# Four graph layers on one Trainium2 core: the turned attention weights of odd tiles are copied out of PSUM by VectorE instead of ScalarE

## The chip, the cores and the metric

The kernel runs on one NeuronCore of a Trainium2 chip. The metric is the device time of one execution in microseconds (us). Five engines work beside each other, each through its own instruction queue in order: TensorE (PE in the profile), VectorE (DVE), ScalarE (ACT), GpSimd (POOL) and SyncE (SP, which issues DMAs here). They wait for each other through semaphores.

## The reference

For each of 8 graphs of 1024 nodes with 128 features, four layers follow each other. Each adds its output to its input and normalizes the rows (layer norm).

```python
x = _layernorm(x + _L0_gnn_ref(adj, x, ...))   # max over the first 25 neighbours, then a linear layer
x = _layernorm(x + _L1_gnn_ref(x, adj, ...))   # graph attention
x = _layernorm(x + _L2_gnn_ref(x, adj, ...))   # graph attention
x = _layernorm(x + _L3_gnn_ref(x, adj, ...))   # attention with logits q x^T, two steps
```

The last layer is the one that the change touches:

```python
mask = jnp.where(dep_adjs == 1, 0.0, NEG)
q = jnp.einsum('bnh,hk->bnk', inputs, att_W)
score = jnp.einsum('bnk,bmk->bnm', q, inputs) / jnp.sqrt(H)
att_adjs = jax.nn.softmax(score + mask, axis=-1)
for W, b in ((W0, b0), (W1, b1)):
    xw = jnp.einsum('bnh,hk->bnk', x, W) + b
    x = jnp.tanh(jnp.einsum('bnm,bmk->bnk', att_adjs, xw))
```

## The kernel before

The 8 graphs are numbered 0 to 7 here. A graph's 1024 nodes are 8 tiles of 128 rows. While graph b goes through its four layers, the neighbour search of graph b+1 (layer 0's maximum) is done in the gaps, by a fixed order written out by hand in each engine's queue. It has two ways for each tile. Some neighbours are gathered from memory: `gather` on POOL issues one indirect DMA a slot (L565), each followed by a small memset as a pause (L570), 18 slots in tiles 0 to 3 and 17 in tiles 4 to 7. They land in a ring of three tile buffers, so a tile's gather waits until the tile three before it has been reduced on DVE (`pool_tile`, L1331 and L1332, `rows_pooled`), and it needs row indices that DVE computes (`find_keys`, `find_members`, `rows_ready`). The other neighbours are "picked" on PE: `pick(b + 1, q)` for q = 0 to 14 is 16 matmuls (L905) with a one-hot matrix that DVE (`make_hot`, L1379) or ACT (`make_hot`, L634 and L637) builds; DVE then takes the maximum (`max_pick`, L1391), which frees the PSUM bank for the next pick. `side_work` runs DVE's share of the search at named places, among them "tile 1" to "tile 5" inside the attention loop, and "steps", "last step", "half" and "end" behind it. In "steps" stand `pool_tile` of tile 4, and `find_keys` and `find_members` of graph b+2. "last step" is `pool_tile` of tile 5, "half" that of tile 6, "end" that of tile 7.

The last layer turns the attention weights tile by tile. For tile t:

- PE multiplies queries by keys into `low` or `high` by turns (L1111) and adds the mask (L1115), and raises `logits_psum`.
- DVE takes the row maximum (L1535), and raises `row_max`.
- ACT takes the exponential with the row sum into `work` (L747, `att_exp`), prepares the mask of tile t+2 (`narrow`, L597), and copies the turned tile t-2 from PSUM (`side_t`) into `probs_t` (L754, `att_t_ready`).
- PE turns tile t-2 with 8 transposes (L1129, `att_turned`) into `side_t`. There is one `side_t`: it must have been copied before the next tile is turned.

PE's order in its loop of 10 steps is: at t = 2 pick 9 and at t = 6 pick 10, the logits of t, then (t = 8, 9) `attend` for two tiles, then the turn of tile t-2. `attend(t)` (L1089) is 8 matmuls that multiply the turned weights with the values. Behind the loop come `attend(4)` to `attend(7)`. Then the first step's result goes through tanh on ACT (L761; it needs `recip`, the reciprocals of the row sums, L1545 on DVE), is turned by `turn_first(0)` and `turn_first(1)` (L1097) with pick 11 around them, is projected (L937), pick 12 follows, and then the second step (L1154) with pick 13 inside, and tanh on ACT (L776). ACT's order behind its loop is: one-hot of pick 11 (L634 and L637, twice), wait for `recip_ready`, tanh. DVE's order behind its loop is: `recip`, "steps", `max_pick` 11, one-hot of pick 12, "last step", `max_pick` 12, and then the residual and statistics of the second step.

Of the kernel before, what the change touches and what calls it, by code (L numbers as in the profile page):

```python
# [19 lines left out]
P = 128  # L20
# [146 lines left out]
def build_graph_layers(nc, x, adj, w0, b0, w1, b1, a1, w2, a2, watt, w3a, b3a, w3b, b3b, out):  # L167
# [13 lines left out]
    with ExitStack() as ctx:  # L181
# [6 lines left out]
        def signal(name, per, unit=1, ahead=0, first=None):  # L188
            return Signal(ctx, nc, name, per, unit, ahead, first)
# [204 lines left out]
        row_max = signal("row_max", T)  # L394
        att_exp = signal("att_exp", T)
        att_turned = signal("att_turned", T)
        att_t_ready = signal("att_t_ready", T)
        recip_ready = signal("recip_ready", 1)
        att_heads = signal("att_heads", 4)
        first_turned = signal("first_turned", 2)  # L400
# [179 lines left out]
        def _(act):  # L580
# [142 lines left out]
            def graph(b, slot, in_loop):  # L723
# [18 lines left out]
                for t in range(T + 2):  # L742
                    if t < T:
                        act.wait_ge(row_max.sem, row_max.at(b, t + 1))
                        if t >= 3:
                            act.wait_ge(att_turned.sem, att_turned.at(b, t - 2))
                        att_exp.raised_by(nc.scalar.activation(work[:, t % 3, :], (low, high)[t % 2], ACT.Exp,  # L747
                                                               bias=neg_max[:, t:t + 1],
                                                               accum_out=row_sum[:, t:t + 1]))
                        if t + 2 < T:  # L750
                            narrow(b, t + 2, place)
                    if t >= 2:
                        act.wait_ge(att_turned.sem, att_turned.at(b, t - 1))
                        att_t_ready.raised_by(nc.scalar.copy(probs_t[:, :, (t - 2) * P:(t - 1) * P], side_t))  # L754
                if exists(b, 1, B, in_loop):
                    make_hot(b + 1, 11)
                act.wait_ge(recip_ready.sem, recip_ready.at(b, 1))
# [71 lines left out]
        def _(pe):  # L829
# [208 lines left out]
            def graph(b, slot, in_loop):  # L1038
# [61 lines left out]
                for t in range(T + 2):  # L1100
                    if t == 2 and exists(b, 1, B, in_loop):
                        spare_maxed(b + 1, 8)
                        pick(b + 1, 9)
                    if t == 6 and exists(b, 1, B, in_loop):
                        spare_maxed(b + 1, 9)
                        pick(b + 1, 10)
                    if t < T:
                        if t >= 2:
                            pe.wait_ge(att_exp.sem, att_exp.at(b, t - 1))
                        for half in halves:  # L1110
                            nc.tensor.matmul((low, high)[t % 2][:, half], queries[:, t * P:(t + 1) * P],  # L1111
                                             xt[:, half], start=True, stop=False, skip_group_check=True)
                        pe.wait_ge(adj_narrowed.sem, adj_narrowed.at(b, t + 1))
                        for half in halves:
                            last = nc.tensor.matmul((low, high)[t % 2][:, half], ident_masked[:, :],  # L1115
                                                    adj_less_1[:, t % 2, half], start=False, stop=True,
                                                    skip_group_check=True)
                        logits_psum.raised_by(last)
                    if t == T:
                        pe.wait_ge(att_exp.sem, att_exp.at(b, T - 1))  # L1120
                    if t >= T:
                        for i in range(2 * (t - T), 2 * (t - T) + 2):
                            attend(i)
                    if t >= 2:
                        pe.wait_ge(att_exp.sem, att_exp.at(b, t - 1))
                        if t >= 3:
                            pe.wait_ge(att_t_ready.sem, att_t_ready.at(b, t - 2))
                        for m in range(T):
                            last = nc.tensor.transpose(side_t[:, m, :], work[:, (t - 2) % 3, m * P:(m + 1) * P],  # L1129
                                                       ident[:, :])  # L1130
                        att_turned.raised_by(last)
                for t in range(4, T):
                    if t == T - 1:
                        pe.wait_ge(att_t_ready.sem, att_t_ready.at(b, T))
                    attend(t)
                turn_first(0)
                if exists(b, 1, B, in_loop):
# [78 lines left out]
        def _(dve):  # L1216
# [290 lines left out]
            def graph(b, slot, in_loop):  # L1507
# [21 lines left out]
                    max_pick(b + 1, 8)  # L1529
                    make_hot(b + 1, 9)  # L1530
                side_work(b, slot, "attention", in_loop)
                for t in range(T + 1):
                    if t < T:
                        dve.wait_ge(logits_psum.sem, logits_psum.at(b, t + 1))
                        row_max.raised_by(nc.vector.tensor_reduce(neg_max[:, t:t + 1], (low, high)[t % 2], AX.X,  # L1535
                                                                  ALU.max, negate=True))
                    if f"tile {t}" in SIDE:
                        side_work(b, slot, f"tile {t}", in_loop)
                    if t == 4 and picks:
                        max_pick(b + 1, 9)  # L1540
                        make_hot(b + 1, 10)
                    if t == T and picks:
                        max_pick(b + 1, 10)
# [106 lines left out]
```

## Time and profile before

| what | value |
| --- | --- |
| median of 3 runs | 1954.62 us (1948.86 to 1959.94) |
| profiled execution | 1953.58 us |
| its span, first to last instruction | 1951.8 us |
| mean granted TensorE clock | 0.94 of full |
| busy share PE, DVE, ACT, POOL | 85%, 72%, 58%, 75% |

The span is what the trace covers; the profiled execution's time is 1.8 us more. A graph takes 225 us in the steady part. Times in rows are counted from the start of the span. The attention loops of graphs 0 to 7 begin near 320, 548, 772, 999, 1223, 1448, 1677 and 1879 us. POOL gathers for graph 7 until 1761 us, and has nothing to do in graph 7 itself.

### The profile page before, as it was taken

The page shows a single profiled execution, that of the slowest core. Times are in us where ns is not written, and L with a number is a line of the kernel's source. Part 1 is how long each engine was busy: PE and PEld are TensorE (multiplying, and loading weights), DVE is VectorE, ACT ScalarE, POOL GpSimd, SP SyncE. Part 2 cuts the span into 40 slices and gives each one's busy share as a digit, 9 for nine tenths or more (in the row PEclk, how much of TensorE's full clock was granted, in tenths as well). Part 3 has the DMA queues.
Part 4 walks back from the last instruction along what each step waited for, and adds up shares of the span by engine and source line. Part 5 has one row for each costly group of instructions (what it writes and reads, how often), then busy time and mean ns, then how long its engine had stood idle before and what let it go on. Part 6 is the DMA issues. An engine that isn't in the chain of part 4 may idle for free.

```text
span 1951.8 us, 29181 instructions
## 1 busy us (share of the span) xinstructions
PE 1666.7 (85%) x9655; PEld 1308.6 (67%) x9700; DVE 1413.3 (72%) x3406; ACT 1126.7 (58%) x1517; POOL 1471.4 (75%) x2191
## 2 busy tenths in 40 slices
PE   4777898979889899899989899997988899896877
PEld 2655675757758577677748677675767687584746
DVE  5874888668876788668885788758886688745631
ACT  5665756646665765657566565558556565652252
POOL 6888888888888887888788887888888887880000
PEclk9989899989999899998999899998999899997889
DMA  7231433343342333334233432434333422311020
GB/s 194 71 83 45 106 75 110 87 107 76 77 131 75 101 78 94 109 91 118 76 115 75 113 78 75 126 77 112 83 101 86 131 55 64 107 43 38 1 65 11
DMA packets 154177, 168.88 MB, mean 87 GB/s; under 512 B 103133, under 2 KB 120426, under 8 KB 154026
## 3 DMA queue, kind: packets, MB, share of 16 engines
q1 hardware_dynamic: 119594, 96.43, 18.2%
q0 software_dynamic: 34432, 70.59, 14.1%
q8 instruction: 76, 1.25, 0.3%
q14 instruction: 75, 0.61, 0.1%
HBM read 142.29 MB, written 4.19 MB: 75 GB/s over the span
## 4 chain that ended last, share of the span: by engine, by line
POOL 32%; PE 31%; DVE 17%; issue 9%; ACT 5%; DVEq 4%; DMA 2%; POOLq 0%; ACTq 0%; SPq 0%
POOL gathered L565 24%; POOL pause L570 8%; PE big L1013 7%; PE spare L905 6%; PE big L937 4%; DVE pooled L1331 3%; DVEq L73 2%; DVE probs_t L1458 2%; PE big L1004 2%; PE big L1154 1%; PE big L1089 1%; DVE keys L1228 1%; ACT hot L634 1%; PE big L1111 1%; PE big L995 1%
## 5 line engine op out<-in xcount | busy, mean ns | idle before, releaser
L565 POOL DMA_INDIRECT gathered<-in_x_dram,rows x1076 | 1107.1, 1029 | 246.9 <-issue 163.3
L905 PE MATMUL spare<-hot,x_part 128*128 128x512 f32 x1440 | 366.7, 407 | 28.5 <-DVE hot L1379 18.9
L570 POOL MEMSET pause<- 32x256 bf16 x1076 | 357.6, 332 | 42.0
L905 PEld LDWEIGHTS spare<-hot,x_part 128*128 128x128 f32 x1440 | 271.3, 194 | 94.7 <-issue 19.4
L634 ACT ACTIVATE hot<-running,minus_count 128x2048 fp32r<-128x2048 bf16 (+1 forms) x131 | 250.8, 1914 | 85.1 <-PE spare L905 65.0
L637 ACT ACTIVATE hot<-hot,plus_one 128x2048 fp32r<-128x2048 f32 (+1 forms) x131 | 251.4, 1919 | 4.3
L1331 DVE TENSOR_REDUCE pooled<-gathered 128x128 f32<-128x2176 f32 (+2 forms) x56 | 218.2, 3897 | 32.0 <-DMA gathered<-in_x_dram,rows 30.5
L1013 PEld LDWEIGHTS big<-values,probs_t 128*128 128x128 f32 x1792 | 224.7, 203 | 8.5
L1013 PE MATMUL big<-values,probs_t 128*128 128x129 f32 x1792 | 227.7, 288 | 0.4
L1379 DVE TENSOR_SCALAR hot<-running 128x2048 fp32r<-128x2048 bf16 (+1 forms) x131 | 167.6, 1302 | 26.5 <-PE big L905 11.7
L1458 DVE SCALAR_TENSOR_TENSOR probs_t<-side,col_gain,adj_t 128x1024 f32<-128x1024 f32 x128 | 154.6, 1276 | 27.2 <-ACT side L693 27.2
L1535 DVE TENSOR_REDUCE neg_max<-big 128x1 f32<-128x1024 f32 x64 | 78.2, 1222 | 99.5 <-PE big L1115 99.5
L615 ACT CAST running<-spare 128x512 bf16<-128x512 f32 x92 | 53.8, 585 | 150.3 <-remote 84.2
L905 PE MATMUL side<-hot,x_part 128*128 128x512 f32 x448 | 115.6, 403 | 26.9 <-DVE hot L1379 16.9
L1111 PE MATMUL big<-xt,queries 128*128 128x512 f32 x256 | 121.1, 595 | 6.5 <-ACT values L679 6.1
L747 ACT ACTIVATE work<-big,neg_max 128x1024 f32<-128x1024 f32 x64 | 71.3, 1114 | 95.1 <-DVE neg_max L1535 95.1
L1089 PE MATMUL big<-values,probs_t 128*128 128x128 f32 x1024 | 118.3, 275 | 0.0
L1154 PEld LDWEIGHTS big<-values,probs_t 128*128 128x128 f32 x1024 | 116.6, 192 | 2.0 <-ACT values L679 0.9
L905 PEld LDWEIGHTS side<-hot,x_part 128*128 128x128 f32 x448 | 80.4, 188 | 55.8 <-issue 16.6
L1154 PE MATMUL big<-values,probs_t 128*128 128x128 f32 x1024 | 116.8, 275 | 0.7 <-ACT values L679 0.7
L1089 PEld LDWEIGHTS big<-values,probs_t 128*128 128x128 f32 x1024 | 116.2, 192 | 0.0
L1391 DVE TENSOR_TENSOR best_t<-best_t,spare 128x512 f32<-128x512 f32 x75 | 51.6, 688 | 77.4 <-PE spare L905 71.2
(203 smaller groups left out, 2613.8 us busy)
## 6 DMA issues: line engine op xcount, KB each, us to landing
adj_in<-in_adj_dram SPq DMA_DIRECT2D x128, 512.0 KB
gathered<-in_x_dram,rows POOLq DMA_INDIRECT x1076, 2.5
xs<-in_x_dram SPq DMA_DIRECT2D x8, 512.0 KB, 4.7
out_dram<-xs SPq DMA_DIRECT2D x8, 512.0 KB, 3.2
adj_t<-adj_bf SPq DMA_TRANSPOSE x64
packed_t<-group_bits SPq DMA_TRANSPOSE x28, 2.7
w_sb<-in_L_gnn_W_dram SPq DMA_DIRECT2D x1, 128.0 KB
w_sb<-in_L_gnn_W_dram SPq DMA_DIRECT2D x2, 64.0 KB
```

Of the source, the lines that this page charges most:

```text
L565: (late_gathered if late else rows_gathered[t % RING]).raised_by(pool.indirect_dma_start(out=gathered[:, t % RING, k * C:(k + 1) * C], out ...
L570: last = nc.gpsimd.memset(pause[quarter:quarter + 32, k // (4 * PAUSED), :], 0.0)
L634: hot_apart.raised_by(nc.scalar.activation(chunk, running[:, tiles[0]:tiles[-1] + 1, :], ACT.Abs, bias=minus_count[:, s:s + 1]))
L637: hot_made.raised_by(nc.scalar.activation(chunk, chunk.bitcast(F32), ACT.Relu, scale=-1.0, bias=plus_one[:, 0:1]))
L905: last = nc.tensor.matmul(pick_bank(b, q), x_parts[part][:, m, :], hot[:, place_of(b, q, m), :], start=(m == 0 and part == 0), stop=(m == ...
L1013: last = nc.tensor.matmul(heads[:, t, 0:C + 1], probs_t[:, j, t * P:(t + 1) * P], values[:, j, :], start=False, stop=(j == T - 1), skip_gr ...
L1089: last = nc.tensor.matmul(low_t[:, t, :], probs_t[:, m, t * P:(t + 1) * P], values[:, m, 0:C], start=(m == 0), stop=(m == T - 1))
L1111: nc.tensor.matmul((low, high)[t % 2][:, half], queries[:, t * P:(t + 1) * P], xt[:, half], start=True, stop=False, skip_group_check=True)
L1154: last = nc.tensor.matmul(low_t[:, t, :], probs_t[:, m, t * P:(t + 1) * P], values[:, m, 0:C], start=(m == 0), stop=(m == T - 1))
L1331: link(nc.vector.tensor_reduce(pooled[:, t, :], rows_of[:, :, 0:n], AX.X, ALU.max))
L1379: hot_ready.raised_by(nc.vector.tensor_scalar(hot_chunk(b, q, c), running[:, tiles[0]:tiles[-1] + 1, :], float(wanted(b, q)), None, ALU.is ...
L1458: gat_probs.raised_by(nc.vector.scalar_tensor_tensor(out=probs_t[:, j, :], in0=gains, scalar=col_gain[:, j:j + 1], in1=adj_t[slot][:, j, : ...
```

## The change

At each odd step t >= 3 of the loop, the copy of tile t-2 is taken from ACT's queue and put into DVE's queue, behind the row maximum of t and ahead of DVE's side work at that step. The semaphore `att_t_ready` becomes two, one for even tiles (raised by ACT) and one for odd tiles (raised by DVE). DVE's loop becomes one step longer: at t = 9 it waits for the turn of tile 7 and copies it, ahead of `recip`.

```diff
-        att_t_ready = signal("att_t_ready", T)
+        att_t_ready = [signal(f"att_t_ready{i}", T // 2) for i in range(2)]
...
-                    if t >= 2:
+                    if t >= 2 and t % 2 == 0:
                         act.wait_ge(att_turned.sem, att_turned.at(b, t - 1))
-                        att_t_ready.raised_by(nc.scalar.copy(probs_t[:, :, (t - 2) * P:(t - 1) * P], side_t))
+                        att_t_ready[0].raised_by(nc.scalar.copy(probs_t[:, :, (t - 2) * P:(t - 1) * P], side_t))
...
                         if t >= 3:
-                            pe.wait_ge(att_t_ready.sem, att_t_ready.at(b, t - 2))
+                            copied = att_t_ready[(t - 3) % 2]
+                            pe.wait_ge(copied.sem, copied.at(b, (t - 3) // 2 + 1))
...
                     if t == T - 1:
-                        pe.wait_ge(att_t_ready.sem, att_t_ready.at(b, T))
+                        pe.wait_ge(att_t_ready[1].sem, att_t_ready[1].at(b, T // 2))
...
-                for t in range(T + 1):
+                for t in range(T + 2):
                     if t < T:
                         dve.wait_ge(logits_psum.sem, logits_psum.at(b, t + 1))
                         row_max.raised_by(nc.vector.tensor_reduce(neg_max[:, t:t + 1], (low, high)[t % 2], AX.X,
                                                                   ALU.max, negate=True))
+                    if t >= 3 and t % 2 == 1:
+                        dve.wait_ge(att_turned.sem, att_turned.at(b, t - 1))
+                        att_t_ready[1].raised_by(nc.vector.tensor_copy(probs_t[:, :, (t - 2) * P:(t - 1) * P], side_t))
                     if f"tile {t}" in SIDE:
                         side_work(b, slot, f"tile {t}", in_loop)
```

## Rows read from the trace of the kernel before

**Rows 1.** Page, the chain of work that ended last, by engine.

```profile
POOL 32%; PE 31%; DVE 17%; issue 9%; ACT 5%; DVEq 4%; DMA 2%; POOLq 0%; ACTq 0%; SPq 0%
```

**Rows 2.** Timeline, POOL: start us, us, instruction, [idle before <- releaser]; tile 4 for graph 4.

```profile
978.51 1.06 POOL L565 DMA_INDIRECT gathered<-in_x_dram,rows  x1 [6.21 <-DVE pooled L1332]
```

**Rows 3.** Timeline, DVE: reduction of tile 7 in graphs 0, 3, 4, 5.

```profile
414.17 3.79 DVE L1331 TENSOR_REDUCE pooled<-gathered 128x128 f32<-128x2176 f32 x1 [8.87 <-DMA gathered<-in_x_dram,rows]
...
1087.95 3.90 DVE L1331 TENSOR_REDUCE pooled<-gathered 128x128 f32<-128x2176 f32 x1 [0.92 <-DMA gathered<-in_x_dram,rows]
...
1315.68 3.90 DVE L1331 TENSOR_REDUCE pooled<-gathered 128x128 f32<-128x2176 f32 x1 [3.78 <-DMA gathered<-in_x_dram,rows]
...
1538.21 3.90 DVE L1331 TENSOR_REDUCE pooled<-gathered 128x128 f32<-128x2176 f32 x1 [3.67 <-DMA gathered<-in_x_dram,rows]
```

**Rows 4.** Timeline, DVE, graph 3: row maxima of tiles 3, 4; last index rows; reciprocals.

```profile
1014.10 1.22 DVE L1535 TENSOR_REDUCE neg_max<-big 128x1 f32<-128x1024 f32 x1
...
1018.29 1.22 DVE L1535 TENSOR_REDUCE neg_max<-big 128x1 f32<-128x1024 f32 x1 [1.34 <-PE big L1115]
...
1027.19 0.26 DVE L1298 TENSOR_SCALAR rows<-row_f,row_base 128x34 uint32<-128x34 f32 x1
...
1035.78 0.20 DVE L1545 RECIPROCAL recip<-row_sum 128x8 f32<-128x8 f32 x1 [0.49 <-ACT work L747]
```

**Rows 5.** Timeline, PE: graph 3's turns of tiles 1, 7, turn_first(0), pick 12; graph 5's turn_first(0).

```profile
1015.04 1.07 PE L1129 MATMUL side<-ident,work 128*128 128x128 f32 x8 [1.56 <-ACT probs_t L754]
...
1042.69 1.04 PE L1129 MATMUL side<-ident,work 128*128 128x128 f32 x8
...
1053.72 0.66 PE L1097 MATMUL side<-ident,work 128*128 128x128 f32 x4 [2.85 <-ACT work L761]
...
1062.35 3.90 PE L905 MATMUL spare<-hot,x_part 128*128 128x512 f32 x16
...
1502.79 0.66 PE L1097 MATMUL side<-ident,work 128*128 128x128 f32 x4 [2.85 <-ACT work L761]
```

**Rows 6.** Lines by form: one-hot on DVE; copies from PSUM on ACT and DVE.

```profile
L1379 DVE TENSOR_SCALAR hot<-running 128x2048 fp32r<-128x2048 bf16 x105 | 127.8, 1245 | 0.3
...
L754 ACT COPY probs_t<-side 128x1024 f32<-128x1024 f32 x64 | 64.2, 1003 | 48.8 <-PE side L1129 48.8
...
L1389 DVE COPY best_t<-spare 128x512 f32<-128x512 f32 x15 | 10.4, 691 | 2.7 <-issue 0.9 <-PE spare L905 0.7
```

**Rows 7.** Timeline, DVE: max_pick 11 in graphs 1, 3, 5.

```profile
609.42 0.69 DVE L1391 TENSOR_TENSOR best_t<-best_t,spare 128x512 f32<-128x512 f32 x1 [8.25 <-PE spare L905]
...
1060.12 0.69 DVE L1391 TENSOR_TENSOR best_t<-best_t,spare 128x512 f32<-128x512 f32 x1 [7.60 <-PE spare L905]
...
1507.61 0.69 DVE L1391 TENSOR_TENSOR best_t<-best_t,spare 128x512 f32<-128x512 f32 x1 [6.67 <-PE spare L905]
```

**Rows 8.** Timeline, ACT, graph 3: the one-hot of pick 11 starts.

```profile
1044.67 2.01 ACT L634 ACTIVATE hot<-running,minus_count 128x2048 fp32r<-128x2048 bf16 x1
```

**Rows 9.** Windows: pick 11 of graphs 3 and 5; the third figure from the end is PEclk.

```profile
1054.00:1060.00 6.00, 6.00 (x24) 4.57 (x22) 0.00 (x0) 1.76 (x5) 4.64 (x7) 0.72 0.17 44
1503.00:1508.00 5.00, 5.00 (x26) 3.61 (x24) 0.39 (x1) 1.83 (x5) 4.26 (x7) 1.00 0.21 52
```

**Rows 10.** Graph 6: last late reduction on DVE; last gather on POOL; median landing.

```profile
1765.32 1.45 DVE L1324 TENSOR_REDUCE pooled<-gathered 128x128 f32<-128x768 f32 x1
...
1760.52 0.95 POOL L565 DMA_INDIRECT gathered<-in_x_dram,rows  x1 [0.16 <-issue]
...
gathered<-in_x_dram,rows POOLq DMA_INDIRECT x1076, 2.5
```

**Rows 11.** Timeline, PE, graph 7: turns of tiles 2 and 3.

```profile
1892.28 1.06 PE L1129 MATMUL side<-ident,work 128*128 128x128 f32 x8
...
1897.02 1.06 PE L1129 MATMUL side<-ident,work 128*128 128x128 f32 x8 [1.53 <-ACT probs_t L754]
```

**Rows 12.** Timeline, POOL, graph 3: a gather during DVE's one-hot of pick 10.

```profile
1022.99 2.29 POOL L565 DMA_INDIRECT gathered<-in_x_dram,rows  x1 [0.16 <-issue]
```

## The prediction, made before the changed kernel was built or run

> **What bounds the kernel now.** I read the page's chain first, then the chain in order of time, then the timelines of PE, DVE, ACT and POOL through the attention of graphs 0, 3, 6 and 7, and last the idle times that stand at the same two places in every graph. The chain gives POOL 32% and ACT only 5% [rows 1]. In order of time it splits each steady graph in two. From the moment DVE reduces tile 1 of the next graph (behind layer 2), POOL gathers tiles 4 to 7 without a gap, for about 107 to 110 us. POOL has waited for that reduction, 6.21 us in this row [rows 2], and it waits at that place in each of the graphs 1 to 6. The whole attention layer lies beside that stretch. It ends when the last rows of tile 7 land and DVE, which is already there, reduces them [rows 3]. From there to the next release of POOL the path is DVE and PE.
>
> So in graphs 0 to 5 the attention costs nothing as long as DVE arrives at tile 7 before its data. The reader should see in [rows 3] how much is left: 8.87 us in graph 0, but only 0.92 us in graph 3 (graphs 1 and 2 are within 0.1 of it), and 3.78 and 3.67 in graphs 4 and 5. A gain in the attention of graphs 0 to 5 is worth nothing, a delay above these margins is paid in full, and it is not given back, since POOL then waits for DVE. In graph 6 the path runs through PE and ACT up to tile 7. Graph 7 has no gathers, and its attention is on the path as a whole.
>
> **What is moved, and its price.** 32 copies leave ACT, 4 a graph, at 1.00 us each [rows 6]. DVE has no copy of this size. Its copy of 512 elements from PSUM takes 0.69, so the bound above is 1.38. Its maximum over 1024 elements from PSUM takes 1.22 [rows 4], which is the nearest row in size and I take it. The bound below is the ACT copy's 1.00.
>
> **Inside the loop.** In graph 3 DVE ends the row maximum of tile 3 at 1015.32 and would go on with side work, but the turn of tile 1 ends at 1016.11 [rows 4, 5]. Wait and copy take it to 1017.33, 2.0 us later. 1.34 us of this was idle before the maximum of tile 4 [rows 4], so 0.7 is left (0.45 to 0.7 over the graphs; I take 0.6). It moves logits, pick 10 and all that follows in the loop. Tiles 3 and 5 have been turned, or nearly, when DVE comes to them; their copies fit into its idle time. DVE's last index rows of the next graph move from 1027.45 to about 1029.4, and POOL asks for them only near 1033 (its tile 6), so that is hidden.
>
> What ACT gives up in the loop is no gain. The chain goes through the copies of tiles 0, 2 and 4, which stay on ACT. Graph 7, where nothing is done beside the loop, shows it: the turn of tile 2 starts without waiting for the copy of odd tile 1, the turn of tile 3 waits 1.53 us for the copy of even tile 2 [rows 11]. With a copy of 1.22 on DVE I walk through the loop of graph 7 and find every later turn where it was. Graph 7: 0.
>
> **Behind the loop: the wait that counts.** DVE reached `recip` at 1035.78. Now it must first wait for the turn of tile 7, which ends at 1043.73 [rows 4, 5], plus 0.6 from above, plus the copy of 1.22: `recip` comes near 1045.6, 9.8 us later. The turn is late since PE does `attend(0)` to `attend(3)` around it. Queued behind it on DVE are `recip`, "steps" (reduction, keys and members), `max_pick` 11, and the one-hot of pick 12. Before, DVE idled 8.25, 7.60 and 6.67 us ahead of `max_pick` 11 in graphs 1, 3 and 5 [rows 7]; graph 2 is like 1, graph 4 like 3. So `max_pick` 11 is late by 1.5, 1.5, 2.2, 2.1 and 3.1 us in graphs 1 to 5. Maximum and first half of the one-hot took 0.69 and 1.25 [rows 6, 7], so that half was ready near 1062.0, and PE started pick 12 at 1062.35 [rows 5]: 0.4 of the delay is absorbed: pick 12 is late by 1.1, 1.1, 1.8, 1.7 and 2.7.
>
> ACT wins on the other side. Without the copy of tile 7 it starts the one-hot of pick 11 near 1040.9 in place of 1044.67 [rows 8], and tanh behind it as much earlier. `recip` at 1045.6 is then not what it waits for. PE's wait of 2.85 us ahead of `turn_first(0)` [rows 5] goes, and PE is through with pick 11 and the projection about 4 us early. It then stands before pick 12 for some 5 us, until DVE has the one-hot. The early ACT is worth nothing here: the stall has moved from 1051 to 1059 and grown.
>
> **The clock.** The wait of 2.85 us before pick 11 was followed by a mean granted clock of 0.72 in graph 3, a part of the stretch at 1.2 GHz and the rest at 2.4, and of 1.00 in graph 5, all at 2.4 [rows 9]. From `turn_first(0)` to `max_pick` 11 it was 6.40 us in graph 3 and 4.82 in graph 5 [rows 5, 7]: 1.6 us is the price of the lower clock. Graphs 1 to 4 and 6 paid it, 0 and 5 did not. The new idle time of 5 us is longer, so I expect the 1.2 GHz behind it in all graphs, now in pick 12, where nothing absorbs it. With 1.6 more the second step is late by 2.7, 2.7, 3.4, 3.3 and 4.3. Less the margins of [rows 3] the tile 7 reduction is late by 1.8, 1.8, 2.5, 0 and 0.6 us in graphs 1 to 5. Graph 0 has 8.87 and nothing is left of its 5: 0. Sum: +6.7.
>
> **Graph 6.** There is no graph 8, so "steps" is only the reduction, and DVE has far more idle time than it loses. PE keeps what ACT gave it: 2.85 - 0.6, and 1.3 since the lower clock goes, 3.6 in all. At its end the last six rows of tile 7 stand in the way: issued at 1760.52 and 2.5 later landed, so near 1763.2, where DVE reduced them at 1765.32 [rows 10]. Gain 2.1 of the 3.6.
>
> Total: +6.7 - 2.1 = +4.6 on the profiled execution's 1953.58 (span 1951.8 and 1.8 around it), 1958.2. The median of the runs is 1.0 above that execution, so the changed kernel's median would be up to 1959.2; I put 1958.5.
>
> **A rule against the change.** A gather of POOL takes 0.95 us, and 2.29 when DVE's one-hot (bf16 in SBUF to SBUF) runs beside it [rows 12]. The rows around DVE's copies and maxima from PSUM show 0.95. If the new copy held POOL like the one-hot, each would cost up to 1.3 us of a POOL that is the bound in graphs 0 to 5. The Trainium skill (SBUF — State Buffer, Who interferes with whom) says that a DVE instruction in a two-port mode locks GpSimd out of the shared port pair, and counts copies among those that can. By that alone the sum would gain the 20 us of the third rival below. The same skill (VectorE: DVE Perf Modes, Why PSUM operands drop a tier) says that a PSUM operand excludes the two-port mode, which agrees with the 0.69 us for 512 elements.
>
> **The rivals.**
>
> - The clock holds (as in graphs 0 and 5): the late pick 12 then costs 1.1, 1.1 and 1.8 against margins of 0.9, and 0 in graphs 4 and 5, some +1.3; with graph 6's -2.1 the time is 1952.8. For it speaks that the same wait of 2.85 was not followed by it twice; against it that it was followed by 1.2 GHz five times and that the wait is now longer. 0.22.
> - The other side, faster: ACT's early start reaches the end, in graph 6 in full, because the last rows land earlier, and graphs 1 to 5 are still POOL's: -3.6, 1950.0. It decides only where DVE's 9.8 us stay below its idle time of 6.7 to 8.3, which they don't. For over 0.5% no path is to be seen, since POOL's stretch does not shrink. 0.04.
> - The copy on DVE locks POOL out: 24 copies in graphs 0 to 5, at 0.6 to 1.3 us, less the margins that this gives DVE: +20, 1974. 0.04.
> - The stall costs more: 1.2 GHz lasts twice as long (3.2 us of cost instead of 1.6), the copy takes 1.38, and one-hots that moved by 2 us meet more gathers at 1.3 us each: +5 to +12 on top, 1963 to 1970. 0.15.
> - My forecast: 0.55.
>
> **The numbers.** Range 1950 to 1969: it holds the forecast, the clock rival, nearly all of the small gain, and most of the heavy stall, and leaves out the port lock. 0.5% is 9.8 us, about what a measurement of this kernel can tell, as the three runs before differ by 11. Faster by that: 0.03. Slower by that (above 1964.4): the port lock, two thirds of the heavy stall and the tail of the forecast, 0.17. Same: 0.80.
>
> **What would show it.** On DVE a wait of some 8 us for the turn of tile 7 ahead of `recip` in all graphs but with little idle time left before `max_pick` 11. On ACT the one-hot of pick 11 about 4 us earlier. On PE the wait before `turn_first(0)` gone, and one of 4 to 6 us before pick 12, with a low clock in it. The reduction of tile 7 in graphs 1 to 3 starting without waiting for DMA, and POOL's wait at tile 4 longer by 2 us. Graph 7 unchanged within 0.5 us. I am wrong if `max_pick` 11 still waits for PE, if POOL's gathers beside L754's successor take over 0.95 us, or if a turn in the loop waits for DVE.

## The result, and the profile after

The changed kernel takes 1967.64 us (median of 6 runs, 1964.31 to 1971.30), beside 1954.49 us for the kernel before in the same rounds (6 runs, 1948.86 to 1959.94). The ratio is 1.0069, with an interval of 1.0049 to 1.0090: slower by 13.2 us, which is more than 0.5%. The forecast was 1958.5 with a range of 1950 to 1969. The range holds the time, near its upper end; the sum of the steps (+4.6 us) is a third of what was lost, and slower by more than 0.5% had been given a chance of 0.17. Every ratio here is taken over the fast runs of both kernels (those within 1.5% of the fastest of the same kernel), so where runs spread widely it is not the quotient of the two medians.

The profiled execution took 1971.3 us. From its page come the span with the instruction count, the busy times, the chain by engine, and the group of the picks (busy time, mean ns of one matmul, idle time before them and its releaser):

```profile
span 1969.5 us, 29181 instructions
...
PE 1682.1 (85%) x9655; PEld 1324.7 (67%) x9700; DVE 1453.1 (74%) x3438; ACT 1098.6 (56%) x1485; POOL 1476.6 (75%) x2191
...
PE 41%; DVE 27%; POOL 12%; issue 7%; ACT 6%; DVEq 6%; DMA 1%; ACTq 0%; POOLq 0%; SPq 0%
...
L905 PE MATMUL spare<-hot,x_part 128*128 128x512 f32 x1440 | 383.4, 420 | 59.0 <-DVE hot L1380 55.1
```

In the chain POOL falls from 32% [rows 1] to 12%, and PE and DVE rise to 41% and 27%. POOL's gathers are no longer what ends last; the attention layer is. PE now stands 55.1 us before the picks until DVE has the one-hot (18.9 before), and a matmul of them takes 420 ns in the mean (366.7 us in all and 407 ns before).

The span is 17.7 us longer. Of this 3.9 us lie ahead of the first row maximum of graph 0 (326.21 in place of 322.36 us), where no instruction was changed: this is how one execution differs from another. From there to the first row maximum of graph 7 it is 1570.69 us instead of 1556.97, and graph 7 itself takes the same time in both.

I read graph 3 next, whose first row maximum is at 1012.55 us here (1002.52 before). DVE, by the timeline (start, us, instruction, idle time before it):

```profile
1024.10 1.22 DVE L1536 TENSOR_REDUCE neg_max<-big 128x1 f32<-128x1024 f32 x1
1026.14 1.22 DVE L1540 COPY probs_t<-side 128x1024 f32<-128x1024 f32 x1 [0.82 <-PE side L1130]
1028.94 1.23 DVE L1536 TENSOR_REDUCE neg_max<-big 128x1 f32<-128x1024 f32 x1
...
1055.92 1.22 DVE L1540 COPY probs_t<-side 128x1024 f32<-128x1024 f32 x1 [6.89 <-PE side L1130]
1057.06 0.19 DVE L1549 RECIPROCAL recip<-row_sum 128x8 f32<-128x8 f32 x1
...
1073.18 0.69 DVE L1392 TENSOR_TENSOR best_t<-best_t,spare 128x512 f32<-128x512 f32 x1
...
1101.55 3.93 DVE L1332 TENSOR_REDUCE pooled<-gathered 128x128 f32<-128x2176 f32 x1
```

Both waits of the forecast are there. DVE waits for the turn of tile 1 and then copies, so that the row maximum of tile 4 begins 16.39 us after the first one, in place of 15.77 [rows 4]. Behind the loop it idles 6.89 us for the turn of tile 7, `recip` comes 44.5 us after the first row maximum (33.3 in [rows 4]), and `max_pick` 11 starts without any idle time, where it had 7.60 [rows 7]. The reduction of tile 7 no longer waits for a DMA ([rows 3] had 0.92): DVE comes 89.0 us after the first row maximum, and the data are there.

PE in the same graph: the turns of tiles 1 to 3, pick 10, the turn of tile 7, `turn_first(0)`, pick 12.

```profile
1025.04 1.07 PE L1130 MATMUL side<-ident,work 128*128 128x128 f32 x8 [1.56 <-ACT probs_t L754]
...
1028.09 1.04 PE L1130 MATMUL side<-ident,work 128*128 128x128 f32 x8
...
1033.49 1.07 PE L1130 MATMUL side<-ident,work 128*128 128x128 f32 x8 [2.21 <-ACT probs_t L754]
1034.81 5.42 PE L905 MATMUL spare<-hot,x_part 128*128 128x512 f32 x16 [0.26 <-DVE hot L1380]
...
1054.85 1.04 PE L1130 MATMUL side<-ident,work 128*128 128x128 f32 x8
...
1062.87 0.60 PE L1097 MATMUL side<-ident,work 128*128 128x128 f32 x4
...
1075.15 5.70 PE L905 MATMUL spare<-hot,x_part 128*128 128x512 f32 x16 [5.03 <-DVE hot L1380]
```

And PE in the kernel before at the turns of tiles 2 and 3 and at pick 10, which the rows ahead of the prediction don't show:

```profile
1018.64 1.06 PE L1129 MATMUL side<-ident,work 128*128 128x128 f32 x8 [0.39 <-ACT probs_t L754]
...
1022.84 1.07 PE L1129 MATMUL side<-ident,work 128*128 128x128 f32 x8 [0.98 <-ACT probs_t L754]
...
1024.16 3.91 PE L905 MATMUL spare<-hot,x_part 128*128 128x512 f32 x16 [0.26 <-DVE hot L1379]
```

The last two rows of each are the find. Ahead of the turn of tile 3, PE waits 2.21 us instead of 0.98, and pick 10, which comes right behind, takes 5.42 us instead of 3.91. The windows over pick 10 and pick 12 show why (columns as in [rows 9], the third figure from the end is the granted clock):

```profile
1034.00:1041.00 7.00, 6.74 (x25) 5.00 (x23) 4.94 (x9) 2.24 (x3) 6.20 (x9) 0.76 0.38 124
1075.00:1082.00 7.00, 6.84 (x28) 5.75 (x29) 6.28 (x5) 2.96 (x2) 6.20 (x9) 0.71 0.80 227
```

The same windows of the kernel before:

```profile
1024.00:1028.00 4.00, 3.83 (x17) 3.20 (x18) 3.37 (x8) 1.68 (x3) 3.60 (x5) 1.00 0.32 114
1062.00:1066.00 4.00, 4.00 (x22) 3.39 (x21) 4.00 (x2) 3.69 (x7) 3.56 (x6) 1.00 0.23 54
```

A mean of 0.76 and of 0.71 means that TensorE was granted 1.2 GHz for part of both picks, where it had 2.4 GHz throughout before.

Two rows for the steps that were expected to hide something. ACT starts the one-hot of pick 11 39.8 us after the first row maximum, 2.3 us earlier than in [rows 8] (42.15). Forecast were 3.8, with 0.6 for the loop already taken off; the loop lost 2.1 here, and 3.8 less the other 1.5 is 2.3. POOL's wait at tile 4 is longer than in [rows 2]:

```profile
1052.38 2.00 ACT L634 ACTIVATE hot<-running,minus_count 128x2048 fp32r<-128x2048 bf16 x1
```

```profile
990.24 1.06 POOL L565 DMA_INDIRECT gathered<-in_x_dram,rows  x1 [8.15 <-DVE pooled L1333]
```

All graphs together, from the same timelines (us; "late" and "after the first row maximum" are counted within the graph):

| | before | after |
| --- | --- | --- |
| row maximum of tile 4 after the first, g0 to g6 | 15.73–15.77 | 16.39–16.58 |
| PE's wait ahead of the turn of tile 3 | 0.98 | 2.20–2.39 |
| pick 10 | 3.9 | 4.9–5.5 |
| row maximum of tile 6 after the first | 27.7 | 29.5–30.1 |
| `recip` after the first | 33.2 | 44.2–44.8 |
| `max_pick` 11 after the first, g0 to g5 | 56.0 or 57.6 | 60.5–61.3 |
| PE's wait before pick 12, and pick 12, g0 to g5 | 0; 3.9 | 5.0–5.5; 5.3–5.7 |
| POOL's release at tile 4 to the reduction of tile 7, g1 to g6 | 109.3, 109.1, 109.4, 110.8, 108.9, 111.1 | 112.6, 112.2, 111.3, 111.4, 111.9, 110.3 |

The last line is the largest part of the loss: +3.3, +3.2, +1.9, +0.6 and +2.9 in graphs 1 to 5, and -0.9 in graph 6, in sum +11.0 of the 13.7 us between graph 0 and graph 7. The stretches behind, from the reduction of tile 7 to POOL's next release, add 4.6, and graph 0 takes 2.3 less up to its tile 7. What the stretches behind depend on is taken up with the fourth group of experiments.

### The profile page after: what moved, and what is told of

Read it like the earlier page. It is cut to its first block, busy times and chain, and to the rows that moved or that the text cites. A ratio compares the mean times of both kernels' runs of the same rounds, so it can differ in the third digit from the quotient of the medians.

```text
span 1969.5 us, 29181 instructions
## 1 busy us (share of the span) xinstructions
PE 1682.1 (85%) x9655; PEld 1324.7 (67%) x9700; DVE 1453.1 (74%) x3438; ACT 1098.6 (56%) x1485; POOL 1476.6 (75%) x2191
## 3 DMA queue, kind: packets, MB, share of 16 engines
q0 software_dynamic: 34432, 70.59, 13.5%
## 4 chain that ended last, share of the span: by engine, by line
PE 41%; DVE 27%; POOL 12%; issue 7%; ACT 6%; DVEq 6%; DMA 1%; ACTq 0%; POOLq 0%; SPq 0%
PE spare L905 10%; POOL gathered L565 9%; PE big L1013 5%; PE big L1155 5%; DVE pooled L1332 4%; PE big L937 3%; POOL pause L570 3%; PE big L1089 3%; DVEq L73 3%; DVE probs_t L1459 3%; PE big L1111 2%; DVE keys L1229 2%; PE side L1130 2%; PE big L1004 2%; PE big L1064 1%
## 5 line engine op out<-in xcount | busy, mean ns | idle before, releaser
L905 PE MATMUL spare<-hot,x_part 128*128 128x512 f32 x1440 | 383.4, 420 | 59.0 <-DVE hot L1380 55.1
L570 POOL MEMSET pause<- 32x256 bf16 x1076 | 365.6, 340 | 42.0
L905 PEld LDWEIGHTS spare<-hot,x_part 128*128 128x128 f32 x1440 | 284.5, 203 | 130.2 <-issue 53.7
L1130 PE MATMUL side<-ident,work 128*128 128x128 f32 x512 | 69.2, 280 | 34.5 <-ACT probs_t L754 34.5
```

Of the source, the lines that this page charges most:

```text
L570: last = nc.gpsimd.memset(pause[quarter:quarter + 32, k // (4 * PAUSED), :], 0.0)
L905: last = nc.tensor.matmul(pick_bank(b, q), x_parts[part][:, m, :], hot[:, place_of(b, q, m), :], start=(m == 0 and part == 0), stop=(m == ...
```

## The experiments

Theory A: there are two stalls. Beside the one that was forecast (DVE waits for tile 7, and PE stalls before pick 12), the copy of tile 1 on DVE makes the row maximum of tile 4 late, PE's wait ahead of the turn of tile 3 grows, and pick 10 runs partly at 1.2 GHz; this one was expected to cost more. Theory B: DVE's wait for the turn of tile 7 is all of the loss. Theory C: each copy on DVE holds POOL up, so their number counts. Theory D, for one run: the slow pick 10 costs over half of the loss whatever stands behind it.

All variants are the changed kernel with the list of tiles that DVE copies made free. `ON_DVE` holds them; `LATE_COPY` says for a tile that its copy stands behind `recip` and before part 0, 1 or 2 of "steps" (the reduction of tile 4, the keys, the members). With (1, 3, 5, 7) and {} it is the changed kernel.

```diff
-                    if t >= 2 and t % 2 == 0:
+                    if t >= 2 and not copier(t - 2):
...
-                    if t >= 3 and t % 2 == 1:
-                        dve.wait_ge(att_turned.sem, att_turned.at(b, t - 1))
-                        att_t_ready[1].raised_by(nc.vector.tensor_copy(probs_t[:, :, (t - 2) * P:(t - 1) * P], side_t))
+                    if t >= 2 and copier(t - 2) and t - 2 not in LATE_COPY:
+                        copy_turned(b, t - 2)
...
-                side_work(b, slot, "steps", in_loop)
+                for part in range(3):
+                    for i, place in LATE_COPY.items():
+                        if place == part:
+                            copy_turned(b, i)
+                    side_work(b, slot, f"steps {part}", in_loop)
```

**First group: parts of the change.** These four ran on a chip on which the kernel before took 2053.55 us in the median of 35 runs (2034 to 2080). In the traces taken there PE often waits for nothing but its own instructions, 14 to 23 us in all at one line (L1025), where the same line idles 0.4 us in the trace of the kernel before. Times that vary by 46 us separate nothing here, but the order of the work within a graph can be read.

```diff
-ON_DVE = (1, 3, 5, 7)
+ON_DVE = (1, 3, 5)
```

> Tiles 1, 3, 5 are copied by DVE, tile 7 by ACT again, so DVE no longer waits for the turn of tile 7 ahead of its side work. Theory A (two stalls: the wait for the turn of tile 7 on DVE, and a slower pick 10 behind a longer wait of PE ahead of the turn of tile 3): the loop's delay of about 2 us a graph stays and goes through PE to the end of the attention, of which about 1 us in graphs 1 to 3 and 2 us in graph 6 exceed the margins, in sum +4 to +6 us, near 1960. Theory B (the wait for the turn of tile 7 is all of it): the time of the kernel before, 1954.5. Theory C (each copy on DVE holds POOL up): three quarters of the loss stay, +10 us, and POOL's gathers last over 0.95 us beside the copies.

2053.24 us, ratio 0.9927 (0.9872 to 0.9982), where Theory A expected about 1.003. The loop was as in the change: row maximum of tile 4 at 16.3 to 16.7 us, the wait ahead of the turn of tile 3 at 2.1 to 2.5. `recip` came at 35 to 37, so DVE's long wait is tied to tile 7 alone.

```diff
-ON_DVE = (1, 3, 5, 7)
+ON_DVE = (7,)
```

> Only tile 7 is copied by DVE. Theory A: pick 10 takes 3.9 us again, recip is 9.2 us later than before, max_pick 11 is 1 to 2.5 us late, pick 12 still starts after a wait of 4 to 5 us and takes about 5.4 us; sum +2 to +4 us, near 1957.5. Theory B: the full loss, +13 us, near 1967.5. Theory C: a quarter of it, +3 us, with recip's delay paying nothing.

2057.29 us, 1.0014 (0.9976 to 1.0053). The counterpart: row maximum of tile 4 at 15.75, the wait at 0.98, pick 10 at 3.9 us, and `recip` at 44 to 45.

```diff
-LATE_COPY = {}
+LATE_COPY = {7: 2}
```

> Tiles 1, 3, 5, 7 on DVE as in the change, but recip, the reduction of tile 4 and the keys of graph b+2 stand ahead of the copy of tile 7, so that DVE hardly waits for it. Theory A: max_pick 11 waits for PE again, pick 12 follows without a wait and takes 3.9 us; graphs 1 to 5 end as before, graph 6 gains up to 2 us: 1952 to 1955, although pick 10 stays slow (5 us). Theory B: the same. Theory C: the full loss stays, near 1967.

2061.76 us, 1.0032 (0.9995 to 1.0068). Inconclusive here; it comes again in the third group.

```diff
-ON_DVE = (1, 3, 5, 7)
+ON_DVE = (3, 5, 7)
```

> Tiles 3, 5, 7 on DVE, tile 1 on ACT as before. Theory A: the row maximum of tile 4 is where it was, PE waits about 1 us instead of 2.3 ahead of the turn of tile 3, pick 10 takes 3.9 us; what is left is the wait for the turn of tile 7: +2 to +4 us, near 1957.5, about 9 us less than the change. Theory B: no difference to the change, 1967. Theory C: three quarters of the loss, +10 us.

2049.12 us, 0.9916 (0.9866 to 0.9967). It too comes again, on a chip where a time means more. That two of the four come out below 1 by 0.7% and 0.8%, and with them one that keeps the slow loop, is no evidence of a gain on such a chip: the medians of all their runs are only 0.02% and 0.2% below the kernel before, and their runs spread over 51 and 50 us.

**Second group: the clock in the loop, and the other tiles.** On this chip the kernel before took 1952.86 us (23 runs). The first kernel is the change, with 14 transposes that nobody reads put on PE ahead of its wait for the copy of tile 2, in graphs 0 to 6. All waits and copies stay; only PE isn't idle in this one.

```diff
+                        if t == 5 and exists(b, 1, B, in_loop):
+                            for _ in range(14):
+                                nc.tensor.transpose(packed[:, 0, 0:P], ident[:, :], ident[:, :])
                         if t >= 3:
```

> The change, plus 14 transposes of the identity on PE (1.5 us, into an unused PSUM bank, not part of the computation) between the logits of tile 5 and the wait ahead of the turn of tile 3, in graphs 0 to 6. Theory A (PE's wait of 2.3 us there is followed by 1.2 GHz in pick 10): the idle time falls under 1 us, pick 10 takes 3.9 us and not 5 to 5.5, everything behind comes 1.3 us earlier in each graph, 5 to 8 us less than the change in sum, near 1960. Theory B (only the wait for the turn of tile 7 counts, the clock does not): no change to the changed kernel, 1967.

1958.88 us (12 runs, 1952.14 to 1963.64), 1.0033 (1.0018 to 1.0048). In all seven graphs pick 10 takes 3.9 us again; the rest of the wait is 0.6 to 0.9 us. The turn of tile 3 and pick 10 of graph 3, and the windows behind the start of pick 10 and of pick 12:

```profile
1024.44 1.09 PE L1145 MATMUL side<-ident,work 128*128 128x128 f32 x8 [0.64 <-ACT probs_t L766]
1025.85 3.92 PE L917 MATMUL spare<-hot,x_part 128*128 128x512 f32 x16 [0.32 <-DVE hot L1395]
```

```profile
1026.00:1032.00 6.00, 5.95 (x24) 4.08 (x26) 4.03 (x9) 2.24 (x3) 5.24 (x8) 1.00 0.31 79
1065.00:1071.00 6.00, 6.00 (x16) 4.70 (x17) 5.21 (x3) 2.31 (x2) 5.33 (x7) 0.57 0.79 231
```

The clock is 1.00 behind the filled wait and 0.57 behind the one that was left empty. The row maximum of tile 6 is at 28.4 to 28.8, that is 0.7 to 1.1 us late, as the forecast had assumed of the change itself; and the cost of 0.33% is near the forecast's (+4.6 us is 0.24%, within the interval). Theory A expected this kernel near 1960, Theory B at 1967. What the filled wait saves, 8.5 us beside the change, is not only pick 10; the fourth group splits it.

The second gives DVE the even tiles, the copy of tile 6 behind `recip` and the reduction of tile 4.

```diff
-ON_DVE = (1, 3, 5, 7)
-LATE_COPY = {}
+ON_DVE = (0, 2, 4, 6)
+LATE_COPY = {6: 1}
```

> DVE copies tiles 0, 2, 4 and 6 in place of 1, 3, 5 and 7; the copy of tile 6 stands behind the reduction of tile 4, and recip ahead of both. Theory A: these are the copies for which PE waited in the kernel before, and DVE can start them sooner than ACT, so the loop is 1 to 2 us shorter; no wait of DVE behind the loop; graphs 0 to 5 are bound by POOL and gain nothing, graphs 6 and 7 gain 1 to 2 us each: 1951 to 1954. Theory C (a copy on DVE holds POOL): as slow as the change, 1965 and more.

1954.72 us (1952.67 to 1959.10), 1.0013 (1.0000 to 1.0026). Graph 7 confirms half of it: the row maximum of tile 6 comes 2 us earlier (18.93 for 20.94), but the turn of tile 7 only 1 us. In graphs 0 to 6 it missed: that row maximum comes 2.6 to 4.2 us later. PE waits 3.3 us for ACT's copy of tile 1 ahead of the turn of tile 2, and 1.2 to 2.9 us for DVE's one-hot before pick 10. DVE, with the neighbour search in its queue, is late for the one-hot. As many copies as in the change cost a fifth of its price or less, and POOL's gathers beside them take 0.95 us, which speaks against Theory C.

**Third group: both waits filled, and the copy of tile 7 put later.** The kernel before took 1968.08 us on this chip (29 runs, 1960.4 to 1980.6), and near pick 11 PE sometimes waits a few us for instructions.

```diff
+                    for _ in range(40):
+                        nc.tensor.transpose(packed[:, 0, 0:P], ident[:, :], ident[:, :])
                     spare_maxed(b + 1, 11)
                     pick(b + 1, 12)
```

> As the warm turn of tile 3, plus 40 transposes of the identity on PE (4.4 us, no part of the computation) ahead of the wait for pick 12 in graphs 0 to 6. Theory A (what is left of the loss is the late pick 12 and the 1.2 GHz behind PE's wait of 5.3 us ahead of it): pick 12 takes 3.9 us and not 5.8, the end of the attention comes 1.8 us earlier than with the first transposes alone, about 1 us short of the margins: another 4 to 6 us less, 1953 to 1955. Theory B (the clock does not matter there, only the wait for the turn of tile 7): no gain over the 1958.9 of the warm turn of tile 3.

That is the kernel with 14 transposes and 40 more before pick 12. 1973.37 us (1961.59 to 1985.09), 1.0024 (1.0000 to 1.0048). Pick 12 took 3.9 us in all graphs. So the mechanism of the clock holds there as well. The time doesn't confirm it: Theory A expected another 4 to 6 us less than with the first transposes alone (1.0033), and 1.0024 with this interval shows no such gain.

> Tiles 1, 3, 5, 7 on DVE as in the change; recip, the reduction of tile 4 and the keys of graph b+2 stand ahead of the copy of tile 7. The same kernel as the one with the copy of tile 7 behind the keys, timed again. Theory A: no wait of DVE for the turn of tile 7, max_pick 11 waits for PE again, pick 12 starts at once and takes 3.9 us; pick 10 stays slow; graphs 1 to 5 end inside their margins: 1950 to 1954, about 14 us less than the change. Theory D (the loop's slow pick 10 alone costs over half of the loss whatever stands behind it): 1960.

This is the kernel with `LATE_COPY = {7: 2}` once more. 1973.49 us, 1.0020 (0.9998 to 1.0043). Now PE is what DVE waits for again (6 to 10 us ahead of `max_pick` 11) and pick 12 takes 3.9 us, while the loop keeps its 2.1 to 2.4 us of wait and, in five of seven graphs, a pick 10 of 4.8 to 5.5 us. In time it decides nothing between the theories: A expected 0.998 to 1.000, D 1.003, and the interval reaches both.

```diff
-ON_DVE = (1, 3, 5, 7)
-LATE_COPY = {}
+ON_DVE = (7,)
+LATE_COPY = {7: 2}
```

> Only tile 7 on DVE, and its copy behind recip, the reduction of tile 4 and the keys. Theory A: neither stall; ACT begins the one-hot of pick 11 some 4 us earlier, PE's wait ahead of turn_first(0) goes; graphs 0 to 5 are POOL's and gain nothing, graph 6 gains up to 2 us: 1950 to 1953, at or just below the kernel before. If POOL did not bound graphs 1 to 5: a gain of 2 us and more in each, below 1945.

1963.61 us, 0.9978 (0.9960 to 0.9996): faster than the kernel before, by little. It differs from the kernel above it only by the copies of tiles 1, 3 and 5, which are on ACT here, and on the same chip it is 9.9 us faster. So these copies cost time on that chip even where the copy of tile 7 holds nothing up.

**Fourth group: side by side on one chip.** The kernel before took 1953.76 us (23 runs, 1947.91 to 1957.21). The change again, the change without the copy of tile 1, and the last kernel of the third group.

> The same instructions as the changed kernel, timed on the same chip as the other two. All theories: 1.0069 of the kernel before, within 1.005 to 1.009.

> Tiles 3, 5, 7 on DVE, tile 1 on ACT, timed again. Theory A (two stalls): PE waits about 1 us ahead of the turn of tile 3 and pick 10 takes 3.9 us; max_pick 11 comes at 60 us behind the first row maximum and pick 12 still takes over 5 us; ratio 1.001 to 1.003, like the changed kernel with the warm turn of tile 3 or a little below. Theory B (only the wait for the turn of tile 7 counts): 1.007, like the change.

> Only tile 7 on DVE, its copy behind recip, the reduction of tile 4 and the keys, timed again. Theory A: faster than the kernel before by what graph 6 gains, 0.998 to 1.000.

| kernel | median, us (range, runs) | ratio to before |
| --- | --- | --- |
| the change | 1967.24 (1960.04–1970.05, 6) | 1.0059 (1.0040–1.0078) |
| tile 1 back on ACT | 1956.49 (1951.08–1960.08, 12) | 1.0012 (1.0000–1.0025) |
| tile 7 alone, behind the keys | 1950.58 (1945.74–1954.11, 12) | 0.9983 (0.9971–0.9996) |

One copy out of four is worth 10.8 of the 13.5 us in time. In the change itself, run again, pick 10 took 4.8 to 5.3 us in graphs 1 to 5 and 3.9 in graphs 0 and 6, pick 12 5.2 to 6.7 in graphs 0 to 5. With tile 1 back on ACT, PE in graph 3 has its turn of tile 3, pick 10 and pick 12 so:

```profile
1025.10 1.06 PE L1142 MATMUL side<-ident,work 128*128 128x128 f32 x8 [0.97 <-ACT probs_t L766]
1026.44 3.89 PE L917 MATMUL spare<-hot,x_part 128*128 128x512 f32 x16 [0.28 <-DVE hot L1392]
...
1065.79 6.53 PE L917 MATMUL spare<-hot,x_part 128*128 128x512 f32 x16 [5.56 <-DVE hot L1392]
```

```profile
1027.00:1033.00 6.00, 6.00 (x28) 4.20 (x27) 4.24 (x9) 2.24 (x3) 5.20 (x9) 1.00 0.32 74
1066.00:1072.00 6.00, 6.00 (x16) 4.67 (x17) 4.98 (x3) 2.33 (x2) 5.20 (x9) 0.55 0.85 221
```

The loop is that of the kernel before (wait 0.97, pick 10 at 3.89, row maximum of tile 4 at 15.76), while behind it stand the stall of the change (5.56 us before pick 12) and a low clock that lasts longer: pick 12 takes 6.3 to 6.5 us in graphs 0 to 5, where it took 5.3 to 5.7 in the change. So Theory B falls, and what was forecast costs 2.7 us net in this kernel. But that is a balance of two larger amounts, which one profiled execution of each kernel shows:

| kernel | attention stretches, graphs 1 to 6, us | stretches behind, graphs 0 to 5, us | L1064 in 3.54 us, of graphs 1 to 6 |
| --- | --- | --- | --- |
| before | 658.6 | 692.6 | 2 |
| the change | 669.6 | 697.2 | 1 |
| the change again | 674.0 | 692.8 | 2 |
| the change, 14 transposes | 668.5 | 687.8 | 4 |
| tile 1 back on ACT | 667.0 | 684.6 | 5 |
| tile 7 alone, behind the keys | 658.0 | 683.1 | 6 |

An attention stretch runs from POOL's release at tile 4 to the reduction of tile 7, the stretch behind from there to POOL's next release. With tile 1 back on ACT the attention stretches still lose 8.4 us, and the stretches behind give 8.0 back. What they hang on is the clock once more, in layer 0 of the next graph. There PE does 16 matmuls at L1064 (L1076 in the variants), in two halves. In graph 2, before and in the last kernel:

```profile
654.99 2.08 PE L1064 MATMUL big<-w_sb,probs_t 128*128 128x128 f32 x8 [0.79 <-DVE probs_t L1512]
...
654.91 1.16 PE L1076 MATMUL big<-w_sb,probs_t 128*128 128x128 f32 x8 [0.78 <-DVE probs_t L1525]
```

From the first of the 16 to the last it takes 3.54 us where 2.4 GHz is granted throughout, 4.87 where it comes back in between (0.64 in graph 2 before) and 5.79 at 1.2 GHz. In the 36 stretches of the table the stretch behind takes 113.1 to 114.7 us with the first of these, and 115.8 to 117.7 with the other two. So of the 10.8 us between the change and the kernel without the copy of tile 1, 2.6 to 7.0 show up in the attention stretches and 8.2 to 12.6 in those behind, in single executions that lie 13.6 and 14.8 us apart. Why the clock of layer 0 comes back in time in one kernel and not in the other no run here shows.

In the last kernel DVE does `recip`, the reduction and the keys first. Its copy of tile 7, `max_pick` 11 and the reduction of tile 7 in graph 3:

```profile
1041.61 1.23 DVE L1590 COPY probs_t<-side 128x1024 f32<-128x1024 f32 x1
...
1050.61 0.69 DVE L1404 TENSOR_TENSOR best_t<-best_t,spare 128x512 f32<-128x512 f32 x1 [2.53 <-PE spare L917]
...
1085.02 3.80 DVE L1344 TENSOR_REDUCE pooled<-gathered 128x128 f32<-128x2176 f32 x1 [7.49 <-DMA gathered<-in_x_dram,rows]
```

The copy waits for nothing, ACT's time is still given back, and DVE is 7.49 us ahead of POOL's data where it was 0.92 ahead [rows 3]. The attention stretches of graphs 1 to 5 don't get shorter by it, as POOL is the bound there (109.6 to 109.8 us; 108.9 to 110.8 before). What this kernel gains is 1.6 us in that of graph 6, and in its profiled execution 9.5 us in the stretches behind, where L1064 takes 3.54 us in all six. This version beats both kernels, by 3.2 us over the one before and 16.7 over the change.

## Why the prediction was right, and where it was off

**What bounds the kernel.** Right, and it carried the rest: the attention of graphs 0 to 5 is hidden behind POOL up to the margins of [rows 3], and paid beyond. Graph 4 had 3.78 us of margin and lost 0.6, graphs 1 to 3 had some 0.9 and lost 3.3, 3.2 and 1.9 (graph 3's stretch has 1.7 us less ahead of the first row maximum than before, 22.3 for 24.0, which is no part of the change). Graph 5 had 3.67 and lost 2.9, since it had run pick 11 at 2.4 GHz before and its `max_pick` 11 is the latest against before, by 5.2. The last kernel shows the other side: 6.6 us more of margin, and these stretches are no shorter. The stretches behind were taken as given, and that was an oversight: they differ by up to 9.5 us in sum between kernels whose instructions are the same there.

**The copy.** 1.22 taken, and 1.224 us in the median of 32. ACT's copies stayed at 1.00.

**Inside the loop.** This is the step that failed: "I take 0.6 … It moves logits, pick 10 and all that follows in the loop." The 0.7 us at the row maximum of tile 4 came nearly as worked out (0.6 to 0.8). What I did not follow was PE's wait ahead of the next turn. Two things add to it. The turn of tile 2 no longer waits for ACT's copy of tile 1 (a wait of 0.39 us before): in graph 3 it begins 3.05 us behind the turn of tile 1 in place of 3.60, so PE is through with it 0.55 earlier. And ACT copies tile 2 behind the exponential of tile 4, which is 0.62 later now. 0.98 + 0.55 + 0.62 is 2.15, and 2.21 was measured (2.20 to 2.39 over the graphs). Of the longer wait only the 0.6 is time lost; the rest of the price came through the clock. Behind it pick 10 ran partly at 1.2 GHz, 1.0 to 1.6 us more. The loop then cost 1.8 to 2.4 us a graph in place of 0.6, on top of margins that the part behind the loop had used up. I had noted that "what ACT gives up in the loop is no gain"; that it was the first half of a loss I did not see. Two runs undo it in different ways: 1956.49 for 1967.24 us without the copy of tile 1, side by side, and 1.0033 for 1.0059 to 1.0069 with the wait filled (on another chip). That shows that the copy of tile 1, through PE's wait, costs most of the time. How the 10.8 us come of 2.2 us in the loop is shown only in part, since most of them appear in the stretches behind and their clock.

**Graph 7: 0.** Right: 72.6 us from its first row maximum to its end, 72.5 before, although `recip` comes 9.2 us later there (35.70 for 26.49). The turn of tile 3 waits 1.56 us, in [rows 11] 1.53: the turn of tile 2 had no wait there that could go, and DVE has idle time ahead of the row maximum of tile 4.

**Behind the loop.** Right in kind. DVE waits for the turn of tile 7 (6.89 us; "some 8" was said, as DVE reached it later), the wait at `turn_first(0)` of [rows 5] is gone, PE stands 5.0 to 5.5 us before pick 12. `max_pick` 11 was late by 3.1, 2.9, 3.0, 2.9 and 5.2 us in graphs 1 to 5, forecast 1.5, 1.5, 2.2, 2.1 and 3.1: the difference is the loop's. Without the loop's part the forecast can be read by itself: its losses of 1.8, 1.8, 2.5, 0 and 0.6 less 0.6 each are 4.3 us, less the 2.1 of graph 6, +2.2; tile 1 on ACT measured +2.7. That these agree is luck. In the stretches that were priced, this kernel's profiled execution lost 9.9 us in graphs 1 to 5 and gained 1.5 in graph 6, with 2.4 to 2.6 us of low clock in pick 12 in place of the 1.6 of the sum; the 8.0 that it gained behind them stood in no term.

**The clock.** Right for pick 12 (5.3 to 5.7 us instead of 3.9, in graphs 0 to 5). The first rival, that the clock holds, fell. That the low clock could strike at a second place, pick 10, or at a third, layer 0, was not in the sum.

**Graph 6.** The sign was right and the size was off: 0.9 gained of 2.1. The last reduction came when POOL's rows landed, as said:

```profile
1782.57 1.45 DVE L1325 TENSOR_REDUCE pooled<-gathered 128x128 f32<-128x768 f32 x1 [2.91 <-DMA gathered<-in_x_dram,rows]
```

DVE was there 2.91 us before them, so it was not the loop that ate the gain. The rows were late: POOL issued its last gather 107.7 us behind its release, where it had been 106.3 in the kernel before, and they landed at 110.2 where the sum had 109.0 (from 1763.2; the prediction's own terms, 1760.52 and 2.5, make 1763.0).

**The port.** The rival of +20 us fell. 41 gathers of POOL ran beside the 32 copies on DVE, and all took 0.95 to 0.96 us, where one beside the one-hot took 2.29 [rows 12]. The trace agrees with the Trainium skill (VectorE: DVE Perf Modes, Why PSUM operands drop a tier): an operand in PSUM keeps DVE out of the two-port mode. That is the mode of the prediction's rule against the change.

**The rival of a heavier stall** (+5 to +12 on top, at 0.15) is where the time came out, but not by its mechanism: in the change the low clock did not last longer at pick 12 (1.4 to 1.8 us of cost), and the copy did not take 1.38 us. The price of the low clock did about double, by a second place in the loop. So that the range holds 1967.64 is in part luck: its upper end stood there for other reasons. The chances say so more plainly than the range: within 0.5% had 0.80, slower by more 0.17, and the latter came. The sum of +4.6 was given too much of the chance, since it left the loop at one number instead of a range.

Left open: with the copy of tile 7 behind the keys but the odd tiles on DVE, the ratios of 1.0020 and 1.0032 come from two chips on which the kernel before is itself slower and uneven; how much of the change's loss that placing alone removes is not settled. The same holds for putting tile 7 alone back on ACT, and for the clock in layer 0: whether a kernel brings it about or an execution falls into it would take more traces of each kernel.

## What to carry to other kernels

When a piece of work leaves an engine, go through every wait of TensorE behind it, those that get shorter too: an engine that is early at one semaphore waits longer at the next, and a wait of 2 us on TensorE can cost another 1.5 in the matmuls behind it. Put a moved copy behind the queued work that others wait for, not ahead of it: the copy of tile 7 with those of tiles 3 and 5, ahead of `recip`, cost 2.7 us, and alone behind the keys it gained 3.2. Once one delay has used up the margin to the bound engine, a further one is no longer hidden, so the smallest term needs the closest reading. And compare a sum with the stretches that it prices, not with the total alone: here a forecast of +2.2 met a measured +2.7 that was 8.4 lost in one place and 8.0 gained in another.

## What the runs showed of the hardware that was not expected

- A wait of 2.2 to 2.4 us ahead of the turn of tile 3 was followed by a stretch at 1.2 GHz in all seven graphs of the change (granted clock 0.76 over pick 10 of graph 3), where the wait of 0.98 us was followed by a pick 10 of 3.9 us in all, at 1.00 in graph 3. But it isn't certain: over the five runs that keep this wait (2.1 to 2.6 us), it was followed by a slower pick 10 in 27 of 35 graphs. When the change was run again, the same wait of 2.25 and 2.27 us in graphs 0 and 6 was followed by a pick 10 of 3.9 us, and with the even tiles on DVE a wait of 2.27 us right before pick 10 was too:

```profile
1024.84 3.91 PE L917 MATMUL spare<-hot,x_part 128*128 128x512 f32 x16 [2.27 <-DVE hot L1392]
```

- Transposes that nobody reads, issued into the wait, kept 2.4 GHz in every graph (pick 10 at 3.9 us, pick 12 at 3.9 us); the row maximum of tile 4 came no later for them (16.4 to 16.7 us).
- In layer 0 of the next graph the 16 matmuls of L1064 took 3.54, 4.87 or 5.79 us by the clock that they were granted, and the whole stretch behind the attention 2.8 us more in the mean where they got 1.2 GHz for a part or all of it (16 of 36).
- The same kernel took 1953, 1968 and 2053 us in the median on different chips; in the traces of its variants PE waits for its own instructions on the last two.
